# Attention: a tile's row sums are transposed behind its own probabilities, into the weighting's bank

## What is computed

```
for l in range(2):
    h = shift_token(x)                       # second half of the columns from the token before
    q, k, v = split(h @ wqkv[l])             # 8 heads of 64
    q = rotary(l2norm(q) * qs);  k = rotary(l2norm(k) * ks)
    # windows of 128 tokens; each attends to its own window and to the one before
    sim  = q k^T, masked to i - 128 <= j <= i
    attn = softmax(sim)
    o    = attn v
    x = x + o @ wo[l]
    x = x + gated_mlp(layernorm(shift_token(x)))
```

## Time and profile before

| | |
|---|---|
| median of 3 runs | 1042.76 us (1042.3 to 1044.64) |
| profiled execution, whole | 1037.41 us |
| its span | 1035.7 us |
| PE busy, share of the span | 953.1 us, 92% |
| PEld | 767.3 us, 74% |
| DVE | 668.4 us, 65% |
| ACT | 514.0 us, 50% |
| POOL | 411.5 us, 40% |
| mean granted clock of PE | 0.984 |

### The profile page before, as it was taken

How to read it: one execution, slowest core, us unless ns; L and a number is a source line. 1 busy time by engine, 2 the same in 40 slices (tenths; PEclk the granted TensorE clock), 3 DMA queues, 4 the chain that set the end, 5 groups by cost and what they waited for, 6 DMA issues and landing times.

```text
span 1035.7 us, 17394 instructions
## 1 busy us (share of the span) xinstructions
PE 953.1 (92%) x5656; PEld 767.3 (74%) x5656; DVE 668.4 (65%) x1686; ACT 514.0 (50%) x1217; POOL 411.5 (40%) x416
## 2 busy tenths in 40 slices
PE   5889969999999988999999889999999999889987
PEld 4668855767676866878787777887787878678876
DVE  6878476357574687666666645577766666645663
ACT  4577731403021325666666554454766666654432
POOL 4233613113120347666666410006675767620030
PEclk9899989999999998999999999999999999999999
DMA  6201013000000000000001020000000000000002
GB/s 244 72 1 61 21 41 107 1 1 1 0 0 1 1 22 1 1 22 0 21 0 30 13 94 20 4 6 20 1 23 0 21 0 18 20 15 17 11 0 85
DMA packets 15172, 26.32 MB, mean 25 GB/s; under 512 B 1098, under 2 KB 11712, under 8 KB 14352
## 3 DMA queue, kind: packets, MB, share of 16 engines
q1 hardware_dynamic: 15120, 25.68, 7.6%
HBM read 20.53 MB, written 2.10 MB: 22 GB/s over the span
## 4 chain that ended last, share of the span: by engine, by line
PE 70%; DVE 9%; ACT 8%; issue 6%; POOL 4%; SPq 2%; DMA 1%; POOLq 0%; ACTq 0%; DVEq 0%
PE bank L1528 30%; PE bank L1862 5%; PE bank L1675 5%; PE bank L1817 5%; PE bank L1723 5%; PE bank L1841 4%; PE bank L1827 4%; ACT probs L1393 4%; PE bank L1804 2%; PE bank L1852 2%; SPq L335 1%; PE bank L1686 1%; POOL scanned L402 1%; PE bank L1594 1%; PE bank L1936 1%
## 5 line engine op out<-in xcount | busy, mean ns | idle before, releaser
L1393 ACT ACTIVATE probs<-bank,row_min 128x256 f32<-128x256 f32 (+1 forms) x256 | 111.6, 462 | 120.8 <-DVE row_min L987 120.8
L534 POOL TENSOR_TENSOR norms<-norms,minus_half 128x16 f32<-128x16 f32 x32 | 93.6, 2924 | 2.7
L987 DVE CUSTOM_DVE_ANT_0 bank<-bank,mask 128x256 f32<-128x256 f32 (+1 forms) x256 | 90.7, 425 | 5.7 <-PE bank L1817 5.6
L1528 PE MATMUL bank<-wqkv_hi,x_hi 128*128 128x512 f32 x192 | 82.6, 430 | 1.8 <-DVE rot L963 1.1
L1528 PE MATMUL bank<-wqkv_lo,x_hi 128*128 128x512 f32 x192 | 76.5, 398 | 0.0
L1528 PE MATMUL bank<-wqkv_hi,x_lo 128*128 128x512 f32 x192 | 76.0, 396 | 0.0
L1124 DVE SCALAR_TENSOR_TENSOR hidden<-bank,lcols,hidden 128x512 f32<-128x512 f32 (+1 forms) x48 | 36.0, 749 | 51.0 <-PE bank L1528 28.3
L1827 PE MATMUL bank<-ident,probs 128*128 128x128 f32 x448 | 61.6, 279 | 3.7 <-ACT probs L1393 3.7
L516 POOL TENSOR_TENSOR q_tok<-rot 128x512 f32<-128x512 f32 x32 | 41.1, 1286 | 57.7 <-DVE rot L963 57.7
L1528 PE MATMUL bank<-t_hi,wm_hi 128*128 128x512 f32 x160 | 63.6, 397 | 0.0
L1528 PE MATMUL bank<-t_lo,wm_hi 128*128 128x512 f32 x160 | 63.6, 397 | 0.0
(11 more groups left out here) (239 smaller groups left out, 2680.2 us busy)
## 6 DMA issues: line engine op xcount, KB each, us to landing
w_stage<-in_wm_l_dram SPq DMA_DIRECT2D x8, 534.0 KB, 3.6
w_stage<-in_wqkv_dram SPq DMA_DIRECT2D x2, 1536.0 KB, 7.7
out_dram<-stream SPq DMA_DIRECT2D x4, 512.0 KB, 3.7
emb<-in_ctx_dram SPq DMA_DIRECT2D x1, 1536.0 KB, 6.9
inner<-in_w_gate_dram SPq DMA_DIRECT2D x1, 1152.0 KB, 10.3
stream<-in_x_dram SPq DMA_DIRECT2D x2, 512.0 KB, 5.8
stream<-in_x_dram SPq DMA_DIRECT2D x1, 1024.0 KB, 12.7
ew<-in_pos_bias_dram SPq DMA_DIRECT2D x1, 1024.0 KB, 11.2
```

The source lines that it names most:

```text
L534: pool.tensor_tensor(norms[:, 2, :], norms[:, 1, :], minus_half[:, :], ALU.pow).then_inc(c_rn, 1)
L987: dve.tensor_tensor_reduce(logits, logits, mask[:, 2 * P - nk:2 * P], 1.0, FAR, ALU.add, ALU.min, row_min[:, w % 2, 2 * i + e:2 * i + e + ...
L1393: act.activation(probs[:, i, e, 0:nk], logits, ACT.Exp, bias=row_min[:, w % 2, h:h + 1], scale=-1.0, accum_out=row_sum[:, w % 2, h:h + 1]) ...
L1528: ins = pe.matmul(out, stationary, moving, start=(first and i == 0), stop=(last and i == len(terms) - 1))
```

## The change

The sums of tile n are transposed in the tile's own window, behind the last transposes of its probabilities, and no longer in the next window behind the scores. They go into bank 3, which the weighting uses, in place of bank 2. ScalarE copies them out behind its last copy of probabilities, and no longer between the fourth exponential and the fifth. The waits change with that: the sums' transposes wait for the normalisation of the tile before (c_ot_out) in place of a residual; the weighting waits for the copied sums (c_rt_out) in place of that normalisation; the keys' transposes wait for the residual of two tiles back in place of the copied sums; the last two projections of a layer wait for the residual before theirs. The sum transposes and the copy behind the last window of a layer are gone, since window 15 has them.

```diff
--- before.py
+++ after.py
@@ -1410,13 +1410,11 @@
 
                 act.wait_ge(c_rt, n + 1)
                 act.wait_ge(c_ot_out, n)
-                act.activation(rsum_t[:, :], bank[2][:, :], ACT.Copy).then_inc(c_rt_out, 1)
+                act.activation(rsum_t[:, :], bank[3][:, :], ACT.Copy).then_inc(c_rt_out, 1)
 
             def window(n, w, l, prev, one, two, three):
                 exps(n, w, 0)
                 exps(n, w, 1)
-                if prev:
-                    sums_transposed(n - 1)
                 exps(n, w, 2)
                 exps(n, w, 3)
                 if two:
@@ -1432,6 +1430,7 @@
                 probs_transposed(n, w, 1)
                 probs_transposed(n, w, 2)
                 probs_transposed(n, w, 3)
+                sums_transposed(n)
                 if two:
                     values(n + 2, (w + 2) % TT)
                 if three:
@@ -1515,7 +1514,6 @@
                         window(n0 + b * TT + w, w % TT, l, True, True, True, True)
                 for w in range(1, TT):
                     window(n0 + NT - TT + w, w, l, True, w < 3, w < 2, False)
-                sums_transposed(n0 + NT - 1)
                 with act.Fori(0, NB - 1) as b:
                     mlp(l * NB + b, l, True)
                 mlp(l * NB + NB - 1, l, False)
@@ -1832,7 +1830,7 @@
 
                 pe.wait_ge(c_pt_out, 4 * n + 4)
                 pe.wait_ge(c_v, n + 1)
-                pe.wait_ge(c_ot_out, n)
+                pe.wait_ge(c_rt_out, n + 1)
                 nk = 2 if w else 1
                 for i in range(KI):
                     for k in range(nk):
@@ -1846,10 +1844,9 @@
             def transpose_sums(n):
 
                 pe.wait_ge(c_rb, n + 1)
-                if not (isinstance(n, int) and n == 0):
-                    pe.wait_ge(c_res, n)
+                pe.wait_ge(c_ot_out, n)
                 for i in range(KI):
-                    ins = pe.transpose(bank[2][:, i * P:(i + 1) * P],
+                    ins = pe.transpose(bank[3][:, i * P:(i + 1) * P],
                                        rsum_heads[:, 2 * i:2 * i + 2, :].rearrange("p e d -> p (e d)"), ident[:, :])
                 ins.then_inc(c_rt, 1)
 
@@ -1858,6 +1855,8 @@
                 pe.wait_ge(c_ot_out, n + 1)
                 if keyed:
                     pe.wait_ge(c_qt, n + 3)
+                else:
+                    pe.wait_ge(c_res, n)
                 for k in range(KI):
                     ins = pe.matmul(bank[2][:, 0:D], o_t[:, k, :], wo_sb[:, k, :], start=(k == 0), stop=(k == KI - 1))
                 ins.then_inc(c_wo, 1)
@@ -1865,13 +1864,12 @@
             def window(n, w, l, prev, one, two, three):
                 score_pairs(n, w)
                 if prev:
-                    transpose_sums(n - 1)
                     weigh_values(n - 1, (w - 1) % TT)
                 if two:
                     qkv(n + 2, (w + 2) % TT, 0)
                     qkv(n + 2, (w + 2) % TT, 1)
                 if one:
-                    transpose_k(n + 1, (w + 1) % 2, [(c_rt_out, n)] if prev else [])
+                    transpose_k(n + 1, (w + 1) % 2, [(c_res, n - 1)] if prev else [])
                 else:
                     pe.wait_ge(c_v, NT * (l + 1))
                     pe.wait_ge(c_rope, 6 * NT * (l + 1))
@@ -1882,6 +1880,7 @@
                     transpose_q(n + 1, (w + 1) % 2)
                 transpose_probs(n, w, 2)
                 transpose_probs(n, w, 3)
+                transpose_sums(n)
                 if two:
                     qkv(n + 2, (w + 2) % TT, 2)
                 if three:
@@ -2001,7 +2000,6 @@
                         window(n0 + b * TT + w, w % TT, l, True, True, True, True)
                 for w in range(1, TT):
                     window(n0 + NT - TT + w, w, l, True, w < 3, w < 2, False)
-                transpose_sums(n0 + NT - 1)
                 weigh_values(n0 + NT - 1, TT - 1)
                 project_o(n0 + NT - 1, False)
                 pe.wait_ge(wm_split, WM_PIECES * NB * (l + 1))
```

## The result

| | before | changed |
|---|---|---|
| median | 1042.45 us (1039.86 to 1044.64, 8 runs) | 1035.21 us (1033.02 to 1037.98, 8 runs) |
| ratio of the two | | 0.9931, 95% interval [0.9915, 0.9947] |
| profiled execution, its span | 1037.41, 1035.7 us | 1033.29, 1031.5 us |
| mean granted clock in it | 0.984 | 0.986 |

The changed kernel is 7.2 us faster, where 3.0 were forecast, with 1037.6 as the low end. The two profiled executions differ by 4.2 us in span. So there are two questions: whether the 3.0 us of moved work are there, and where the rest of the 7.2 is.

What follows compares the result with a forecast made beforehand. In w≠0 windows ScalarE's block up to the keys' copy, then PE, sets the period; in w=0 PE does. Terms 0.8 + 0.9 - 0.9 + 0.9 - 0.1 + 1.4 = 3.0 us, 1042.8 to 1039.8; range 1037.6 to 1042.6.

Steps and rivals of the forecast that it cites:

- first window: First window of each layer: no old sums to drop but its own added, -0.44 each, -0.9 us in all.
- ten windows w≠0: Windows not on a first tile: 0.48 off ScalarE's block minus 0.44 for moved transposes, 0.04 each, 0.8 us over 20.
- three windows w=0: First tiles' windows (n = 4, 8, 12), paced by PE: 0.58 minus 0.44, taken as 0.15, 0.9 us over 6.
- window 14: Window without qkv: VectorE's wait on the row-sum copy goes, q's transposes 0.9 earlier, less 0.44; 0.45 a layer, 0.9 us.
- window 15 and tail, to the MLP's first matmul: Layer's end: window 15 loses 0.05 each, the last weighing no longer waits for a residual, gaining 0.7 a layer.
- q transposes at 8.32: In w≠0 windows q's transposes start 8.32 us after the scores in place of 8.80, following ScalarE's copy of the keys.
- sum transposes of 0.43 us without a wait on GpSimd: At their new place the sum transposes take 0.44 us; GpSimd's spread lands with 1.9 us of cover.
- the direct change from 64x128 to 128x64: PE's array shape step, taken to cost as one change; at double price the w=0 term is 0.
- the estimate for ScalarE's copy: ScalarE's row-sum copy at 0.52 us by the skill page, giving 0.08 in place of 0.04 a w≠0 window.
- Rival B: The clock: the fall to 1.2 GHz behind window 14's idle gap goes, another 1.5 us off, 1038.3; chance 0.15.
- C: Something else holds ScalarE's block, w≠0 windows gain nothing or lose 0.05, shape change costs double: 1042.5; chance 0.20.
- D: Slower: sum transposes cost 0.59 at the new place, ScalarE gives back only 0.45: 1045.2 us; chance 0.08.

Runs made afterwards that it cites:

- filler: 12 matmuls whose results nobody reads, on PE ahead of the keys' transposes in windows 14; 1039.20 us on the kernel before, 1035.82 on the changed kernel.
- before_again: The kernel before, run once more with no edit: 1042.06 us (12 runs).
- before_fill: The kernel before with 12 unread matmuls on PE in the gap of window 14 of each layer: 1039.20 us, ratio to before 0.9981.
- after_again: The changed kernel, run once more with no edit: 1034.21 us (6 runs), ratio to before 0.9926.
- after_fill: The changed kernel with the same 12 unread matmuls in windows 14: 1035.82 us, ratio to before 0.9951.
- after_gap: The changed kernel with one more VectorE product ahead of the normalisation in windows 14, for a longer PE gap: 1039.49 us, ratio to before 0.9964.
- copy_first: The kernel before with ScalarE's copy of the old row sums put ahead of its first exponential, PE's order unchanged: 1034.41 us, ratio 0.993.
- the best version: The changed kernel with sum transposes ahead of q's, except in windows 14 and 15, plus 12 unread matmuls in windows 14: 1024.05 us, ratio 0.9834.

## Why the forecast was wrong

**The terms of the work were right.** Layer 1, whose windows had no fall in either profile:

| term (gain in us) | forecast | measured in layer 1 |
|---|---|---|
| first window | -0.44 | 8.92 to 9.38: -0.46 |
| ten windows w≠0 | 0.40 | 135.49 to 135.16: 0.33 |
| three windows w=0 | 0.45 | 36.52 to 36.05: 0.47 |
| window 14 | 0.45 | 12.19 to 11.59: 0.60 |
| window 15 and tail, to the MLP's first matmul | 0.65 | 16.90 to 16.29: 0.61 |
| sum | 1.5 | 1.55 |

Twice 1.55 is 3.1, against 3.0. Layer 0, from the profiles of the two kernels with filler, which have no fall in windows 14, gives 327.64 to 325.96 us from its first scores to those of layer 1: 1.68. The reading behind it held point by point: q transposes at 8.32, PE's wait there of 0.15 us (0.3 was forecast) and 1.01 (1.1), sum transposes of 0.43 us without a wait on GpSimd, the direct change from 64x128 to 128x64 at the price of one change (q transposes 0.58 us earlier in w=0, of the 0.58 that were moved). One change of shape less was worth its 0.15 us (12.18 to 12.03 in w=0). By the Trainium skill (TensorEngine Tiling (Array Packing), "Key Properties") a change of mode drains the array. The windows agree in that a change costs time; no row shows the drain itself. By the Trainium skill (ScalarE: Activation LUTs, "What ACT_TABLE_LOAD costs") the estimate for ScalarE's copy was 0.52 us. The row has 0.48; with 0.52 a w≠0 window would have become 0.08 us shorter, and it became 0.03 shorter.

The term that was undersized most is window 14, by 0.15. The normalisation follows right behind VectorE's last mask and came 5.01 us after the scores in place of 6.10 (904.50 - 898.40 before, 899.84 - 894.83 after, in layer 1), 1.09 earlier. The forecast had taken the 0.95 us of idle time in front of it for the whole; idle time is counted from the end of the row before, and rows of one engine overlap, so a start can move by more than that. PE's gap shrank by 0.52 us, where 0.4 was forecast.

**The step that failed is the one from the profile to the median**: "the difference is carried over unchanged: 1042.8 - 3.0 = 1039.8". The 5.35 us between the profiled execution and the median of before were no constant outside the span. The profiled execution was at 0.984, the executions of this kernel have 0.981 in the mean and go down to 0.978, and each 0.001 is 0.93 us: 2.8 us of the 5.35 go with the clock in this way, and the profiled execution lies 1.6 below the line besides, which is not explained. The row to doubt stood in the table of times, 1037.41 below the lowest of the three runs, 1042.3. That gap was in part a loss that the change takes away in many executions, for the mean clock of the changed kernel's first 8 is 0.984. In part it is a loss that the change cannot touch: 2.6 us more ahead of the attention in before_again's profile than in the first.

**Rival B was the right mechanism and had the wrong size and chance.** It gave 1.5 us, for the one window 14 that had fallen in the profile, and 0.15. The profile of before shows one fall and one escape after equal gaps of 3.06 us, which should have been read as: either can fall in any execution. The filler took 2.0 to 3.2 us off before, the longer gap added 2.8 to 4.1 to the changed kernel beyond its delay. Against that rival stood "the runs of before need not all have had it"; their distance from the profiled one was a reason to think that many had more falls than it.

C and D (nothing gained in w≠0 and the shape change at double price; the new place at 0.59) are refuted by the rows: q transposes 0.47 us earlier in w≠0, windows of 12.03 in w=0, and the 0.43.

**What stays open.** 1035.2 against 1042.45 is 7.2. Work accounts for 3.1 by the windows, the filler for 2.0 to 3.2 more, and the changed kernel with filler is 0.6 to 1.6 above the one without, where no difference was expected. So the remaining 1 to 2 us are within the scatter of these medians, or are falls elsewhere. Falls elsewhere there are: ahead of the attention, and in window 15 of layer 1 in the profiles of before_fill, after_again, after_fill and after_gap, behind waits of 0.73, 0.74 or 1.22 us. Only profiles show where the clock fell, one for each run, so how the falls of the timed executions are spread over these places is not known. At one and the same mean clock the changed kernel's executions lie 3.8 to 5.0 us below those of before (at 0.984: 1034.48, the mean of 7, against 1038.92, the mean of 7), which is more than the 3.1 of work. 0.001 of mean clock does not cost the same everywhere (5.1 us for 0.007 between the two profiles of the changed kernel, 0.73 for 0.001, where the line has 0.93), so this is no contradiction, but it was not traced. Why copy_first's clock fell behind 1.96 us and the changed kernel's mostly held behind 2.54 was not settled.

## What to carry to other kernels

Where windows with unequal work on the busiest engine last equally long, look for the other engine's unbroken block that sets the period; what is moved from ahead of that wait to behind it is paid in full, and what is moved into the wait is free (here 0.03 us won in a w≠0 window by the former, in the mean, and 0.35 in a w=2 window by the latter). Before a sum made on a profiled execution is set against a median, put the execution's granted clock and its time beside those of the runs: where they differ, the difference is not a constant, and the change may touch part of it. A gap of PE that is sometimes followed by the lower clock costs more than its length, and filling it with useless matmuls is a cheap test, and was also a gain in two of the three kernels tried. The profile of the test shows whether the falls went or only moved.

## What the runs showed of the hardware that was not expected

The same instructions take more or less time from one execution to the next, by the clock that PE is granted: 1036.74 to 1045.01 us in 42 executions of one kernel, along 0.93 us for 0.001 of mean clock. In the eleven profiles the same code ahead of the attention ends anywhere between 387.63 and 392.60 us, and a window 14 lasts 12.19 us or 13.68 to 13.73, and 14.90 where 12.2 was due. Twelve matmuls more in each layer made the kernel before faster by 3.2 us by the medians (2.0 by the ratio), and the best version by 4.7 (3.8). The fall does not follow from the length of the gap alone: after 3.06 us the clock fell in layer 0 and held in layer 1 of one execution, after 1.96 it fell, after 2.54 it held in both layers, and in window 15 it fell behind a wait of 0.73 us in after_again and after_fill and held in the first profile of the changed kernel.
